# No barrier between the first and the second pass: the last eight first-pass steps written in turn with the first eight of the second

## The reference

```python
# x, ctx: (128, 128, 256); mask: (128, 128, 128); 16 heads of 16
x = x + tanh(g_xattn[0]) * attention(layernorm(x), ctx, ctx)            # no weights
x = x + tanh(g_ffn[0])   * fp8_matmul(layernorm(x), kernel) + ...       # 256 x 256
x = x + tanh(g_xattn[1]) * masked_attention(layernorm(x) @ Wq.T + bq,
                                            ctx @ Wk.T + bk, ctx @ Wv.T + bv) @ Wo.T + ...
xn = layernorm(x) * gamma + beta
scale = max(abs(xn)) / 127            # over the whole tensor
x = x + tanh(g_ffn[1])   * (round(xn / scale) * scale) @ ternary(W).T
```

## Time and profile before

| | |
|---|---|
| median of 3 runs | 2208.81 us (2200.94 to 2210.47) |
| the profiled execution | 2196.41 us, of it 2194.6 us from first to last instruction |
| granted TensorE clock, mean | 0.968 of full speed |
| busy | PE 89%, DVE 82%, ACT 75%, POOL 58% |
| first pass | to 835.1 us: a step is about 5.9 us in the loop |
| second pass | from 835.2 us: a step is about 9.3 us in the loop |

### The profile page before, as it was taken

How to read it: one execution, slowest core, us unless ns; L and a number is a source line. 1 busy time by engine, 2 the same in 40 slices (tenths; PEclk the granted TensorE clock), 3 DMA queues, 4 the chain that set the end, 5 groups by cost and what they waited for, 6 DMA issues and landing times. The chain is left out here.

```text
span 2194.6 us, 74425 instructions
## 1 busy us (share of the span) xinstructions
PE 1954.8 (89%) x24736; PEld 1431.9 (65%) x24736; DVE 1805.6 (82%) x3446; ACT 1649.6 (75%) x2631; POOL 1274.5 (58%) x2417
## 2 busy tenths in 40 slices
PE   3889898898898975999999999899999999999756
PEld 2666666666666654777677777677777777777445
DVE  4689899999899975788888888788888888888379
ACT  1788888888888872777677777677777777777479
POOL 2688888888888862355555555455555555555300
PEclk7999999999999996999999999999999999999689
DMA  2222222222222200000000000000000000000035
GB/s 81 66 68 65 66 68 67 65 69 67 65 66 67 64 19 27 22 21 23 22 23 22 22 22 20 21 22 20 21 20 22 22 22 22 22 22 15 1 118 189
DMA packets 113889, 95.53 MB, mean 44 GB/s; under 512 B 13441, under 2 KB 113793, under 8 KB 113793
## 3 DMA queue, kind: packets, MB, share of 16 engines
q1 hardware_dynamic: 113792, 94.23, 14.1%
HBM read 60.63 MB, written 33.55 MB: 43 GB/s over the span
## 5 line engine op out<-in xcount | busy, mean ns | idle before, releaser
L864 DVE TENSOR_REDUCE a_nmax<-bank_max 128x8 f32<-128x1024 f32 x512 | 623.3, 1217 | 111.5 <-DVEq L863 110.3
L1130 PE MATMUL bank_max<-UM,U 32*128 32x256 f32 x4096 | 587.6, 404 | 21.3 <-PEq L1243 14.3
L1137 PE MATMUL bank_exp<-UM,U 32*128 32x256 f32 x4096 | 560.3, 390 | 3.9 <-PEq L1278 3.4
L663 ACT ACTIVATE probs<-bank_exp 128x1024 f32<-128x1024 f32 x256 | 262.5, 1025 | 286.7 <-ACTq L662 286.7
L1130 PEld LDWEIGHTS bank_max<-UM,U 32*128 32x128 f32 x4096 | 354.5, 186 | 113.8 <-issue 107.4
L1152 PE MATMUL bank_o<-probs,V 128*17 128x128 f32 x8192 | 326.5, 276 | 102.8 <-PEq L1148 95.8
L545 POOL TENSOR_SCALAR UM<-U,heads_eo 128x512 f32<-128x512 f32 x128 | 88.9, 694 | 545.8 <-POOLq L543 545.8
L1137 PEld LDWEIGHTS bank_exp<-UM,U 32*128 32x128 f32 x4096 | 374.6, 186 | 7.3 <-issue 6.4
L1152 PEld LDWEIGHTS bank_o<-probs,V 128*17 128x17 f32 x8192 | 192.0, 96 | 258.9 <-issue 257.8
L962 DVE CAST bank_max<-ff_qT 128x1024 f32<-128x1024 bf16 x256 | 314.3, 1228 | 23.0
L590 ACT ACTIVATE probs<-bank_exp 128x1024 f32<-128x1024 f32 x256 | 262.4, 1025 | 62.8 <-ACTq L589 47.8
(11 more groups left out here) (166 smaller groups left out, 4286.1 us busy)
## 6 DMA issues: line engine op xcount, KB each, us to landing
X<-in_x SPq DMA_DIRECT2D x128, 128.0 KB, 2.1
ctx<-in_ctx SPq DMA_DIRECT2D x128, 128.0 KB, 2.0
out_y<-U SPq DMA_DIRECT2D x128, 128.0 KB, 1.7
ctx<-out_y SPq DMA_DIRECT2D x128, 128.0 KB, 2.1
out_y<-X SPq DMA_DIRECT2D x64, 256.0 KB, 2.1
ff_qq<-in_mask_BxSxS_ik SPq DMA_DIRECT2D x128, 64.0 KB, 1.8
X<-in_L_xattn_Wq SPq DMA_DIRECT2D x1, 256.0 KB, 3.0
X<-in_L_xattn_Wk SPq DMA_DIRECT2D x1, 256.0 KB, 3.3
```

The source lines that it names most:

```text
L663: nc.scalar.activation(a_probs[n], exp_pair[:, :, :, :].rearrange("p i h t -> p (i h) t"), ACT.Exp, scale=SCALE).then_inc(act_own, 1)
L864: return v.tensor_reduce(a_nmax[:, k2, n * H // 2:(n + 1) * H // 2], max_pair[:, :, :, :].rearrange("p i h t -> p (i h) t"), axis=AX.X, op ...
L1130: last = mm(max_pair[:, r % 2, 2 * c:2 * c + 2, :], U[now][32 * r:32 * r + 32, c, :], UM[now][32 * r:32 * r + 32, DC + c, :, :], start=not ...
L1137: last = mm(exp_pair[:, r % 2, 2 * c:2 * c + 2, :], U[before][32 * r:32 * r + 32, DC + c, :], UM[before][32 * r:32 * r + 32, c, :, :], sta ...
```

## The change

The barrier goes on all five engines. `steps` writes the first pass up to a(128) only; then the new function `both_passes` writes, on PE, DVE, ACT and POOL, a(129), b(-5), a(130), b(-4) and so on to a(136), b(2); the second pass goes on alone from b(3). SP keeps its order without the barrier. What this needs: `xn_T`, `mask_i` and `mask_b` get tiles of their own; the priming matmuls and the wait for them move into b(-5); DVE's two first pairs of statistics wait for `stats_read`; PE waits in b(-1) and b(1), before the V product, for a new semaphore `y_freed`, since V and the pair's product share `bank_m`; and POOL settles V in all steps, so that SP can wait for `slot_used` before the first four context loads of the second pass.

```diff
-        xn_T = [spare[:, n * D:(n + 1) * D].rearrange("p (c t) -> p c t", c=DC) for n in range(2)]
+        xn_T = [sb(f"xn_T{n}", [P, DC, P], FP32)[:, :, :] for n in range(2)]
...
-        mask_i = [ff_qq[:, n, :].bitcast(I32) for n in range(2)]
-        mask_b = [ff_qT2[:, n, :] for n in range(RING)]
+        mask_i = [sb(f"mask_i{n}", [P, P], I32)[:, :] for n in range(2)]
+        mask_b = [sb(f"mask_b{n}", [P, P], BF16)[:, :] for n in range(RING)]
...
+        A_ALONE = NB + 1
+        AB = A_ALONE + 5
+        B_ALONE = A_HI - AB
...
+        def both_passes(run_a, run_b, close=lambda: None):
+
+            for i in range(A_ALONE, A_HI):
+                run_a(i, i % UNROLL, lambda off: 0 <= i + off < NB)
+                close()
+                run_b(i - AB, (i - AB) % UNROLL, lambda off: 0 <= i - AB + off < NB)
+                close()
...
-            sp.drain().then_inc(pass_ends[0], 1)
-            sp.wait_ge(pass_ends[0], 5)
...
-                    if live(0):
-
+                    if not live(0):
+                        sp.wait_ge(slot_used, 1)
+                        sp.sem_inc(slot_used, -1)
+                    else:
                         sp.wait_ge(ctx_done, 1)
                         sp.sem_inc(ctx_done, -1)
...
+                    y_ins = nc.scalar.activation(a_y[(k + 7) // 2 % 2].rearrange("p b n -> p (b n)"), bank_m[:, :],
+                                                 ACT.Copy, scale=scales[:, 3:4])
+                    if live(-5):
+                        y_ins.then_inc(y_out, 1)
+                    else:
+
+                        y_ins.then_inc(act_own, 1)
+                        act.wait_ge(act_own, 1)
+                        act.sem_inc(act_own, -1)
+                        act.sem_inc(y_out, 1)
+                        act.sem_inc(y_freed, 1)
...
-            steps(step_a, A_LO, A_HI, A_FIRST, A_LAST, pe)
-            pe.drain().then_inc(pass_ends[0], 1)
-            pe.wait_ge(pass_ends[0], 5)
-
-            for b in bank_max + bank_exp:
-                last = mm(b, ident[:, :], ident[:, :].rearrange("p (o t) -> p o t", o=1).broadcast_to([P, HG, P]),
-                          start=True, stop=True, skip_group_check=True)
-            last.then_inc(primed, 2)
+            steps(step_a, A_LO, A_ALONE, A_FIRST, A_LAST, pe)
...
+                if live(5) and not live(4):
+                    for b in bank_max + bank_exp:
+                        last = mm(b, ident[:, :], ident[:, :].rearrange("p (o t) -> p o t", o=1)
+                                  .broadcast_to([P, HG, P]), start=True, stop=True, skip_group_check=True)
+                    last.then_inc(primed, 2)
...
+                if live(1) and not live(-2) and (k + AB) % 2 == 1:
+
+                    pe.wait_ge(y_freed, 1)
+                    pe.sem_inc(y_freed, -1)
...
-            steps(step_b, B_LO, B_HI, B_FIRST, B_LAST, pe)
+            both_passes(step_a, step_b)
+            steps(step_b, B_ALONE, B_HI, B_FIRST, B_LAST, pe)
```

More of the change, by code:

```diff
@@ L219, in build @@
         y_out = sem("y_out")
+        y_freed = sem("y_freed")
         attn_x = sem("attn_x")
@@ L494, in step_a @@
                                                     gate[:, 0:1], 0.0, ALU.mult, ALU.add)
[L495 to L501, removed]
+                    mine(v_ins)
+                    settle()
+                    pool.sem_inc(v_made, 1)
+                    pool.sem_inc(slot_used, 1)
                 if live(0):
@@ L510, in _ @@
             hand_back()
-            steps(step_a, A_LO, A_HI, A_FIRST, A_LAST, pool, hand_back)
-            pool.drain().then_inc(pass_ends[0], 1)
-            pool.wait_ge(pass_ends[0], 5)
+            steps(step_a, A_LO, A_ALONE, A_FIRST, A_LAST, pool, hand_back)
             def step_b(i, k, live):
@@ L559, in step_b @@
                     split_shift(k % 2)
-            steps(step_b, B_LO, B_HI, B_FIRST, B_LAST, pool, hand_back)
+            both_passes(step_a, step_b, hand_back)
+            steps(step_b, B_ALONE, B_HI, B_FIRST, B_LAST, pool, hand_back)
             pool.wait_ge(scale_in, 1)
@@ L645, in step_a @@
                     copy_attn()
[L647 to L652, removed]
+            steps(step_a, A_LO, A_ALONE, A_FIRST, A_LAST, act)
             def seed_exp(ring):
@@ L673, in step_b @@
                 odd = k % 2 == 1
+                if live(5) and not live(4):
+                    act.wait_ge(primed, 1)
+                    act.sem_inc(primed, -1)
                 if live(-2):
@@ L727, in step_b @@
                     copy_attn()
-            steps(step_b, B_LO, B_HI, B_FIRST, B_LAST, act)
+            both_passes(step_a, step_b)
+            steps(step_b, B_ALONE, B_HI, B_FIRST, B_LAST, act)
             act.drain().then_inc(pass_ends[1], 1)
@@ L951, in step_a @@
                     vec.sem_inc(stats_made, 1)
[L953 to L958, removed]
+            steps(step_a, A_LO, A_ALONE, A_FIRST, A_LAST, vec, hand_back)
             def seed_max(ring):
@@ L968, in step_b @@
                 s, n = (k + 1) // 2 % 2, (k + 1) % 2
+                if live(5) and not live(4):
+                    vec.wait_ge(primed, 1)
+                    vec.sem_inc(primed, -1)
                 if live(-4):
@@ L1005, in step_b @@
                                     ALU.add).then_inc(u_made, 1)
-                if odd and (live(5) or live(-5)) and (live(1) or live(-9)):
+                if odd and live(5) and not live(1):
+                    vec.wait_ge(stats_read, 1)
+                    vec.sem_inc(stats_read, -1)
+                elif odd and (live(5) or live(-5)):
                     vec.wait_ge(pair_read, 1)
@@ L1038, in step_b @@
                     seed_max((k + 1) % RING)
-            steps(step_b, B_LO, B_HI, B_FIRST, B_LAST, vec, hand_back)
+            both_passes(step_a, step_b, hand_back)
+            steps(step_b, B_ALONE, B_HI, B_FIRST, B_LAST, vec, hand_back)
             v.tensor_reduce(nmax[:, 0:1], absmax[:, :], axis=AX.X, op=ALU.max).then_inc(scale_in, 1)
```

2 lines of the change are left out of this document (removed).

## The result

| | before | changed |
|---|---|---|
| median of four runs | 2209.64 us (2200.94 to 2212.56) | 2177.64 us (2169.55 to 2204.83) |
| ratio | | 0.9846, 95% interval 0.9817 to 0.9875 |
| the profiled execution | 2196.41 us | 2204.83 us |

All ratios leave out runs that are more than 1.5% above the fastest of their kernel: here the one of 2204.83 us, in the comparison with e1 to e4 one of the kernel before (2221.27 us), and in e3 three of six.

What follows compares the result with a forecast made beforehand. Between the passes no engine was the bound, but a chain going from engine to engine. 13.1 us earlier less 0.65 us gave about 12.4 us, from the median of 2208.81 us to 2196.4 us, range 2184 to 2206 us.

Steps and rivals of the forecast that it cites:

- first scores: PE's first scores of the second pass, b(0): 0.65 us of the gain lost there, leaving them 12.4 us earlier.
- U: The bias addition on DVE ahead of b(0)'s first scores: starts at 833.8 us instead of 846.89 us, 13.1 us earlier.
- The priming: Four PE matmuls moved ahead of a(130)'s attention transpose: about 1.0 us at full clock, some 2.06 us at half.
- The subtraction of a(134): On DVE behind b(0)'s first seed: takes 0.69 us, delays the transpose and first scores, 0.65 us back.
- the prediction's own sign: Prediction wrong if the distances at b(3) and the end differ by over 1 us, or it is under 9 us.
- R1: Rival: clock back sooner, one or two of three half-clock projections at full; gain 14.2 or 16 us, 2193 to 2195 us; chance 0.16.
- R2: Rival: the two passes' chains hold each other up, 5.1 us lost, gain 7.3 us, 2201.5 us; chance 0.15.
- one more projection at half clock: A loss counted in R2: a second-pass projection of sixteen matmuls on PE at half clock, 1.8 us.
- the low stretches: Half-clock stretches on PE before the first projection and b(1): would shorten with less PE idle; not in the sum.
- The bare additions of R2: Pair work of a(134) to a(136) beside b(0) to b(2), not hidden in waits: 2.9 us lost.
- a difference worked out in it is carried over to the median: The 12.4 us from the profiled execution (2196.41 to 2184.0 us) taken off the median 2208.81 us, giving 2196.4 us.
- R4: Rival: a missed wait still joins the passes, the projection waits as before, 2208.8 us; chance 0.04.

Runs made afterwards that it cites:

- e1: The kernel before with the second pass's hardware loop at four steps a turn instead of eight, on all engines: 2181.82 us, ratio 0.9928.
- e4: The changed kernel with 32 already met waits (16 instructions) added at the start of PE's program: 2224.82 us, ratio 1.0113 to the kernel before.
- e3: The changed kernel run once more, unchanged, for the spread of its runs: 2205.20 us, ratio 0.9969 to the kernel before.
- e10: The kernel before with four steps a turn in the second pass's loop, run again as the base of a later call: 2182.20 us.
- e12: The changed kernel with four steps a turn in the second pass's loop, run again in a later call: 2171.82 us.
- e6: The kernel before with 240 already met waits added at the start of PE's program: 2209.82 us.

## Why the prediction was wrong

**The mechanism was right, and its sum held up to the first scores.** Each step of the walk, with 2.08 us added back to the times of the changed kernel:

| step | foretold | measured |
|---|---|---|
| reciprocal behind a(130)'s transpose | 0.4 us late | 0.35 us |
| end of the third scaling of a(131) | 823.8 us | 823.60 us |
| subtraction of a(132) | 825.5 us | 825.39 us |
| ACT's copy of the pair | 827.05 us | 827.01 us |
| POOL's shift and scale for b(-3) | 825.3 to 827.1 us | 825.09 to 827.26 us |
| first projection | 829.9 us | 829.71 us |
| U | 13.1 us earlier | 13.3 us |
| first scores | 12.4 us earlier | 12.25 us |
| DVE's wait ahead of U | about 4 us | 2.84 us |

The priming, at full clock, took the 1.0 us foretold (1.03 us); at half clock, in the kernel before, its four matmuls took 1.89 us and not the 2.06 us of the prediction, as they overlap.

The subtraction of a(134) stood right behind the seed, at 833.32 us, and took 1.07 us instead of 0.69 us, while POOL worked beside it; with that the first scores lost 1.05 us, for 0.65 us foretold. DVE's wait ahead of U was shorter than foretold, since the mask row ahead of it took 1.28 us (0.21 us before) beside POOL's addition; that cost nothing. At the end of the program the worth is 11.9 us (e1, e2) and 10.4 us (e10, e12), for 12.4 us foretold. That it comes so near is in part luck: in the traces of e1 and e2 the distance is 12.6 us at the first maximum, ACT's returns add 1.9 us that no term of the sum has, and the clock behind the last maximum takes 2.6 us off. By the prediction's own sign it was wrong in both pairs: from b(3) to the end the distance goes from 12.9 to 11.7 us (e1, e2) and from 9.9 to 7.9 us (e10, e12), where it allowed a difference of 1 us and no less than 9 us.

**R1 fell, R2 half came true.** The first scores of b(0) took 2.08 us and the projection of b(1) 2.08 us for its first eight matmuls: the clock was at half where it had been full before (1.16 us for those eight). It had risen meanwhile and fell again:

```profile
832.00:835.00 3.00, 0.99 (x7) 0.55 (x6) 2.96 (x6) 0.77 (x2) 1.36 (x2) 0.90 0.22 68
835.00:837.00 2.00, 2.00 (x10) 1.18 (x8) 0.85 (x2) 1.57 (x3) 0.00 (x0) 0.50 0.03 8
```

PE worked 0.99 us in the 3 us before, while DVE had the subtraction of a(134) to do. That is the term of R2, one more projection at half clock. By the rule of the Trainium skill, "TensorE: Matmul & The Clock Gate", Part 1, that activity releases the clock, the prediction had the low stretches shorten. At the first projection they didn't, though a transpose and the pair product stood right ahead of it: its first eight matmuls took 2.04 us, for 2.05 us before. Up to b(8) e12 took 3.2 us more than e10, e2 no more than e1 (75.7 and 76.0 us). The bare additions of R2 didn't come: DVE still waited 1.05 to 1.54 us ahead of its maxima in b(1) and b(2).

**The step that failed** is the one in which "a difference worked out in it is carried over to the median", and the range with it. I took the 14 us by which the runs before spread as a width without a cause. The cause stood in the trace of before: two returns of the loop with 9.9 us lost, some 7 us of PE's idle time on L1130 at them, and 18 packets more on the instruction queue than the program is long. With some 5 us for each place, and e1 and e2 as the kernels without any, the first four runs of the changed kernel had about 0, 1, 3 and 7 of them and those of before 4 to 6; that is an estimate, as only the profiled executions were counted, and it can be one too high: by the same sum the profiled execution of before would have three, and it has two and 4.9 us of the clock at the end. The 32 us of the first comparison are then 12 us of the change and some 20 us of luck, of which e3 took back more than all. A forecast from the profile should have had 2174 us as its low end, 2196.4 less 9.9 and 12.4 us: no place at all. Even that is above the two fastest of the first four runs, 2169.55 and 2172.94 us; the clock at the end, 5 us either way, was the second thing that the range didn't hold.

R4 fell with the first trace. On the kernel as it stands the change's 12 us can't be told from the returns of the loop, which put 41 us between two runs of the changed kernel; on e1 they are clear, as its six runs lie within 1.7 us and those of e2 within 4.4 us.

**A better version.** e2 is the changed kernel with four steps a turn: 2169.90 and 2171.82 us in the two calls, at most 2173.74 us in a run, where the changed kernel had 2169.55 to 2210.43 us and the kernel before 2183.76 to 2221.27 us. Against before it is 0.9875 (0.9831 to 0.9919) and 0.9843 (0.9820 to 0.9866).

## What to carry to other kernels

Where runs of one kernel spread by more than a few tenths of a per cent, find what they spread over before a change is judged: the distance from step to step, and the instruction queue's packets against the length of the program, show it in one trace. A hardware loop of 1826 instructions on PE is too long here, one of 1450 isn't; of a loop that is unrolled for its ring of buffers, unroll no more than the ring. Two chains of hand-overs that idle every engine are worth laying side by side, and a walk with the old rows gave the gain within some tenths up to the first scores. At the first maximum the barrier between them was the small part (2.5 of 13 us); over whole runs its absence was 5.9 of 10.4 us, 2.0 us of them for ACT's returns. A loop return can also cost a little on an engine that nobody suspects: compare the last step of a turn with the others.

## What the runs showed of the hardware

- PE's loop of 1826 instructions was fetched anew at 2 to 13 of its 13 returns in the seven traces that have it (by their times, the fastest runs had none; that is an estimate). Each such return had nine packets of 16 KB and took 4.6 to 5.1 us in the mean of a trace (6.4 us in e6; one alone 2.7 to 7.1 us), with PE standing still for up to 4.5 us. A loop of 914 or 1450 instructions was never fetched anew.
- Sixteen instructions added far ahead of the loop took it from seven to thirteen such returns; 64 did the same, 240 gave six.
- After such a stand the granted clock was at 0.59 for 4 us, which is a part of the 5 us.
- ACT's return of its loop cost 0.07 us a turn in the kernels with the barrier and nothing in those without it.
- Where the second pass empties, one kernel had a granted clock of 0.73 in one execution and 0.50 in another, and 5.5 us between them.
- 240 waits that are already met, at the start of PE's program, made the kernel 15 us longer; 64 of them cost 0.2 us (first maximum at 44.07 us for 43.89 us), as they lay in PE's wait for the weights. So each takes more than the 63 ns that 15 us in 240 would give (an estimate).
